# Mixture-of-experts attention block: another order of work in the attention stage, and fewer register instructions in the expert stage

## The reference, cut to what matters

```
x = x + conv(groupnorm(x))                      # untouched by the change
t = x as (8, 256, 64)
n = layernorm(t)
t = t + softmax((n Wq' + bq)(n Wk' + bk)' / 8) (n Wv' + bv)
n = layernorm(t)
p = softmax(n gate_w + gate_b); the two largest, divided by their sum, are the shares
t = t + sum over the two experts e of share_e * (silu(n w1[e]) * (n w2[e])) w3[e]
```

## Time and profile before

| what | before |
|---|---|
| median of 3 runs | 532.63 us (531.43 to 534.22) |
| profiled execution | 531.87 us |
| its span, first to last instruction | 530.1 us |
| mean granted clock of TensorE | 0.761 of full speed |
| busy: TensorE, VectorE, ScalarE, GpSimd | 373.8, 272.1, 181.0, 165.5 us |

### The profile page before, as it was taken

How to read it: one execution, slowest core, us unless ns; L and a number is a source line. 1 busy time by engine, 2 the same in 40 slices (tenths; PEclk the granted TensorE clock), 3 DMA queues, 4 the chain that set the end, 5 groups by cost and what they waited for, 6 DMA issues and landing times.

```text
span 530.1 us, 8806 instructions
## 1 busy us (share of the span) xinstructions
PE 373.8 (71%) x2739; PEld 201.0 (38%) x2739; DVE 272.1 (51%) x559; ACT 181.0 (34%) x401; POOL 165.5 (31%) x179
## 2 busy tenths in 40 slices
PE   0799999999999999998476261705046666666670
PEld 0533534344443434332355150604024444444440
DVE  3569877997789787789325433223112222122222
ACT  3746557464656565630133120101012222222220
POOL 2443232324233242300102435151503333333331
PEclk9969999999999999999786767555555555555555
DMA  9599999896949577670000000000022322232224
GB/s 290 203 215 287 220 279 264 219 222 158 214 126 211 139 172 184 154 206 1 0 0 2 13 8 16 6 16 5 21 65 70 74 72 69 66 71 68 71 48 119
DMA packets 55093, 61.52 MB, mean 116 GB/s; under 512 B 22900, under 2 KB 35244, under 8 KB 54928
## 3 DMA queue, kind: packets, MB, share of 16 engines
q1 hardware_dynamic: 52528, 58.93, 43.4%
q0 software_dynamic: 2528, 2.14, 1.3%
HBM read 11.95 MB, written 11.83 MB: 45 GB/s over the span
## 4 chain that ended last, share of the span: by engine, by line
SPq 13%; PE 12%; issue 9%; DMA 5%; DVE 5%; POOL 5%; ACT 1%; POOLq 0%; ACTq 0%
POOL rows L1226 4%; DMA x_in<-rows 4%; SPq L989 3%; SPq L988 3%; SPq L992 3%; SPq L985 2%; SPq L993 2%; PE ps_go L1388 2%; PE ps_s L1434 2%; PE ps_xv L1350 1%; PE ps_go L1443 1%; DVE ln_out L1030 1%; PE ps_xv L1426 1%; POOL ln_rstd L1211 1%; DMA both<-parts 1%
## 5 line engine op out<-in xcount | busy, mean ns | idle before, releaser
L684 DVE TENSOR_TENSOR prod<-ps_t,a_rep 128x1024 f32<-128x1024 f32 x128 | 152.0, 1218 | 35.8 <-PE ps_t L384 34.9
L384 PE MATMUL ps_t<-b,vt 32*128 32x512 f32 x512 | 75.4, 659 | 1.9 <-DVE prod L684 1.9
L1235 POOL DMA_INDIRECT parts<-y_sb,x_in x47 | 45.7, 972 | 92.6 <-ACT y_sb L1308 92.2
L791 POOL TENSOR_TENSOR a<-a,mask 128x512 f32<-128x512 f32 (+1 forms) x40 | 47.0, 1177 | 83.9 <-ACT a L544 81.9
L404 PE MATMUL ps_d<-prod,keep 128*32 128x512 f32 x512 | 69.1, 612 | 0.3 <-DVE prod L684 0.2
L1426 PE MATMUL ps_xv<-attention_pack,x_in 128*128 128x128 f32 x47 | 22.3, 475 | 57.9 <-DMA x_in<-rows 57.9
L325 PEld LDWEIGHTS ps_m<-om_r,sel 128*128 128x128 f32 x193 | 29.0, 188 | 75.5 <-ACT mask L522 28.2
L1140 DVE COPY xs<-ps_xv 128x128 f32<-128x128 f32 x47 | 13.7, 292 | 79.3 <-PE ps_xv L1426 79.3
L1300 ACT ACTIVATE gated<-ps_s 128x128 f32<-128x128 f32 x47 | 13.0, 278 | 108.3 <-PE ps_p L1435 108.3
L1226 POOL DMA_INDIRECT rows<-stage,slot_at x32 | 31.6, 988 | 57.6 <-DVE stage L1106 35.7
L325 PE MATMUL ps_m<-om_r,sel 128*128 128x256 f32 x193 | 49.3, 334 | 0.0
(11 more groups left out here) (151 smaller groups left out, 530.3 us busy)
## 6 DMA issues: line engine op xcount, KB each, us to landing
a_rep<-a SPq DMA_DIRECT2D x128, 256.0 KB, 4.8
rows<-blank SPq DMA_DIRECT2D x8, 1056.0 KB, 7.8
w_in<-in_experts SPq DMA_DIRECT2D x47, 96.0 KB, 1.9
a_rep<-a SPq DMA_DIRECT2D x32, 128.0 KB, 3.4
x_in<-rows SPq DMA_DIRECT2D x47, 33.0 KB, 1.8
x_in<-rows SPq DMA_DIRECT2D x47, 32.0 KB, 1.7
start<-in_start SPq DMA_DIRECT2D x1, 1344.0 KB, 7.3
both<-parts SPq DMA_DIRECT2D x4, 256.0 KB, 3.6
```

The source lines that it names most:

```text
L384: mm = pe.matmul(out, vt[par][r, v % 2, :, :, :].rearrange("p j y c -> p (j y c)"), b[par][r, pair_taps(v // 2), :].rearrange("p t x -> p ...
L684: dve.tensor_tensor(p[:, :, :], t[:, :, :], a_rep[par][:, ms, pair_taps(v // 2), :].rearrange("p m t x -> p m (t x)"), ALU.mult).then_inc( ...
L791: pool.tensor_tensor(v, v, mask[(PAIRS * par + k) % 2][:, 0:wide, :], ALU.mult).then_inc(a_done, 1)
L1235: pool.indirect_dma_start(out=parts[:, :], out_offset=bass.IndirectOffsetOnAxis(ap=x_in[b][:, C + ROW - 1:C + ROW].bitcast(I32), axis=0), ...
```

## The change

The rounds are gone. Each engine has a list written by hand, in which a couple's phases are interleaved more finely. GpSimd computes the four roots of s = 0 first, and the root of s = 1 for couple q + 1 ahead of the scatters of couple q. Moments, variances and roots have a place for each couple, so `power` waits no longer for `ln_apply`. The two copies into `stage` are ScalarE's (`keep`). `qkv` and `project_qkv` are split in two, `copy_qk` and `copy_v`, `project_qk` and `project_v`, so that each half has its own place in a list. The scatters of the rows have no bounds check; those of the results take theirs from a register that is set once. SyncE reads four steps' values with one load for each row of the table (`table_values`, `LOADS` = 4), and without the check of their range. The order of SyncE's three loads within a step is the same, and they were all SyncE's before.

```diff
-    ROUNDS = COUPLES + 2
+    LOADS = 4
...
-        moments = [sb(f"ln_moments{s}", [P, K, 2]) for s in two]
+        moments = [sb(f"ln_moments{s}", [P, COUPLES, K, 2]) for s in two]
...
+        def table_values(eng, line, s, most):
+            ahead = min(LOADS, STEPS - s)
+            return nc.values_load_multi_w_load_instructions(
+                table[line:line + 1, s:s + ahead], engines=(eng.engine,), min_val=0, max_val=most,
+                skip_runtime_bounds_check_because="the table's entries are clamped where they are made")[1]
...
         @block.sync
         def _(sp):
+            sp.wait_ge(tab_done, 1)
+            sp.wait_ge(placed, 16 * 2 * TT)
             for s in range(STEPS):
                 b = s % RING
-                if s == 0:
-                    sp.wait_ge(tab_done, 1)
-                    sp.wait_ge(placed, 16 * 2 * TT)
-                expert_row = sp.value_load(table[1:2, s:s + 1], min_val=0, max_val=(EXPERTS - 1) * P)
+                if s % LOADS == 0:
+                    at_rows, at_expert = table_values(sp, 0, s, DEAD), table_values(sp, 1, s, (EXPERTS - 1) * P)
+                row = at_rows[s % LOADS]
                 if positive(s - RING + 1):
                     sp.wait_ge(y_ps, s - RING + 1)
-                sp.dma_start(w_in[b][:, :], w_rows[bass.ds(expert_row, P), :]).then_inc(w_here[b], 16)
-                row = sp.value_load(table[0:1, s:s + 1], min_val=0, max_val=DEAD)
+                sp.dma_start(w_in[b][:, :], w_rows[bass.ds(at_expert[s % LOADS], P), :]).then_inc(w_here[b], 16)
                 if positive(s - RING + 1):
                     sp.wait_ge(sent[b], 16 * (uses(s) - 1))
...
```

VectorE's list (`ln` is stats, moments and variance; `largest` score_max and score_negate; `residual` invert_sums and add_values; `choose` gate_logits to top_hot; `place` top_slot and top_share):

```diff
+            ln(0, 0)
+            ln(0, 1)
+            ln_apply(0, 0)
+            ln(0, 2)
+            ln_apply(0, 1)
+            ln(0, 3)
+            largest(0)
+            ln_apply(0, 2)
+            residual(0)
+            ln(1, 0)
+            largest(1)
+            ln_apply(1, 0)
+            ln_apply(0, 3)
+            choose(0)
+            residual(1)
+            ln(1, 1)
+            largest(2)
+            ln_apply(1, 1)
+            place(0)
+            choose(1)
+            residual(2)
+            ln(1, 2)
+            largest(3)
+            ln_apply(1, 2)
+            place(1)
+            choose(2)
+            residual(3)
+            ln(1, 3)
+            place(2)
+            ln_apply(1, 3)
+            choose(3)
+            place(3)
             step_table()
```

GpSimd:

```diff
             def power(s, q):
                 pool.wait_ge(ln_stat[s], LN_STEPS * (q + 1))
-                if positive(q):
-                    pool.wait_ge(ln_done[s], q)
...
             def place(q):
-                pool.wait_ge(ln_done[1], q + 1)
-                for i in two:
-                    k = K * q + TPI * i
-                    pool.tensor_copy(stage[:, k:k + TPI, :, 0:C], spread(normed[1][:, :, i, :], 2, 2)).then_inc(staged, 1)
                 pool.wait_ge(staged, 2 * (q + 1))
...
-                            in_=stage[:, k, w, :], in_offset=None, bounds_check=DEAD - 1, oob_is_err=False)\
+                            in_=stage[:, k, w, :], in_offset=None)\
                             .then_inc(placed, 16)
...
-                    in_=y_sb[b][:, :], in_offset=None, bounds_check=2 * TT * P - 1, oob_is_err=False)\
+                    in_=y_sb[b][:, :], in_offset=None, bounds_check=last_part, oob_is_err=False)\
...
+            for q in range(COUPLES):
+                power(0, q)
+            power(1, 0)
+            power(1, 1)
+            place(0)
+            power(1, 2)
+            place(1)
+            power(1, 3)
+            place(2)
+            place(3)
+            last_part = pool.snap(2 * TT * P - 1)
             for s in range(STEPS):
                 send(s)
```

ScalarE's new `keep`, and its list from couple 0's attention on (`weights` is exps, `turned_weights` copy_p):

```diff
+            def keep(q):
+                act.wait_ge(ln_done[1], q + 1)
+                for i in two:
+                    k = K * q + TPI * i
+                    act.activation(stage[:, k:k + TPI, :, 0:C], spread(normed[1][:, :, i, :], 2, 2), ACT.Copy)\
+                       .then_inc(staged, 1)
...
+            weights(1)
+            turned(1, 0)
+            turned_weights(1)
+            copy_qk(2)
+            copy_v(2)
+            keep(0)
+            gap_exps(0)
+            turned(0, 3)
+            copy_qk(3)
+            weights(2)
+            turned(1, 1)
+            turned_weights(2)
+            copy_v(3)
+            keep(1)
+            gap_exps(1)
...
```

TensorE's list (after it, as before, `counts()` and the steps):

```diff
+            turn(0, 0)
+            project_qk(0)
+            project_v(0)
+            scores(0)
+            turn(0, 1)
+            project_qk(1)
+            turn_p(0)
+            values(0)
+            scores(1)
+            project_v(1)
+            turn(0, 2)
+            project_qk(2)
+            turn(1, 0)
+            project_v(2)
+            turn_p(1)
+            gate_product(0)
+            values(1)
+            scores(2)
+            rank(0)
...
+            scores(3)
+            rank(1)
+            turn(1, 2)
+            turn_p(3)
+            gate_product(2)
+            values(3)
+            rank(2)
+            turn(1, 3)
+            gate_product(3)
+            rank(3)
             counts()
```

More of the change, by code:

```diff
@@ L844, in token_stage @@
         stats = [sb(f"ln_stats{s}", [P, K, 6]) for s in two]
-        moments = [sb(f"ln_moments{s}", [P, K, 2]) for s in two]
-        var_eps = [sb(f"ln_var{s}", [P, K]) for s in two]
-        rstd = [sb(f"ln_rstd{s}", [P, K]) for s in two]
+        moments = [sb(f"ln_moments{s}", [P, COUPLES, K, 2]) for s in two]
+        var_eps = [sb(f"ln_var{s}", [P, COUPLES, K]) for s in two]
+        rstd = [sb(f"ln_rstd{s}", [P, COUPLES, K]) for s in two]
         normed = [sb(f"ln_out{s}", [P, TPI, 2, C]) for s in two]
@@ L966, in token_stage @@
         w_rows = d["experts"]
-        def stages(r):
-            return [q if 0 <= q < COUPLES else None for q in (r, r - 1, r - 2)]
+        def table_values(eng, line, s, most):
[3 more added lines that the diff above has]
+                skip_runtime_bounds_check_because="the table's entries are clamped where they are made")[1]
         def uses(s):
@@ L1014, in ln_moments @@
                 for k in range(K):
-                    dve.bn_aggr(moments[s][:, k, :], stats[s][:, k, :]).then_inc(ln_stat[s], 1)
+                    dve.bn_aggr(moments[s][:, q, k, :], stats[s][:, k, :]).then_inc(ln_stat[s], 1)
             def ln_variance(s, q):
                 dve.wait_ge(ln_stat[s], LN_STEPS * q + 2 * K)
-                dve.tensor_scalar(var_eps[s][:, :], moments[s][:, :, 1], LN_EPS, None, ALU.add)\
+                dve.tensor_scalar(var_eps[s][:, q, :], moments[s][:, q, :, 1], LN_EPS, None, ALU.add)\
                    .then_inc(ln_stat[s], 1)
@@ L1029, in ln_apply @@
                     i, t = divmod(k, TPI)
-                    op = dve.tensor_scalar(normed[s][:, t, i, :], t_tok[:, K * q + k, :], moments[s][:, k, 0:1],
-                                           rstd[s][:, k:k + 1], ALU.subtract, ALU.mult)
+                    op = dve.tensor_scalar(normed[s][:, t, i, :], t_tok[:, K * q + k, :], moments[s][:, q, k, 0:1],
+                                           rstd[s][:, q, k:k + 1], ALU.subtract, ALU.mult)
                 op.then_inc(ln_done[s], 1)
@@ L1153, in finish @@
                 dve.tensor_tensor(tokens, added[q][:, :, :], tokens, ALU.add).then_inc(finished, 1)
-            dve.wait_ge(pack_in, 16)
[L1156 to L1185, removed]
@@ new lines, in ln, with largest, residual, choose @@
+            def ln(s, q):
+                ln_stats(s, q)
+                ln_moments(s, q)
+                ln_variance(s, q)
+            def largest(q):
+                score_max(q)
+                score_negate(q)
+            def residual(q):
+                invert_sums(q)
+                add_values(q)
+            def choose(q):
+                gate_logits(q)
+                top_largest(q)
+                top_index(q)
+                top_hot(q)
+            def place(q):
+                top_slot(q)
+                top_share(q)
@@ L1208, in power @@
                 pool.wait_ge(ln_stat[s], LN_STEPS * (q + 1))
-                if positive(q):
-                    pool.wait_ge(ln_done[s], q)
-                pool.tensor_tensor(rstd[s][:, :], var_eps[s][:, :], minus_half[:, :], ALU.pow)\
+                pool.tensor_tensor(rstd[s][:, q, :], var_eps[s][:, q, :], minus_half[:, :], ALU.pow)\
                     .then_inc(ln_pow[s], 1)
             def place(q):
-                pool.wait_ge(ln_done[1], q + 1)
-                for i in two:
-                    k = K * q + TPI * i
-                    pool.tensor_copy(stage[:, k:k + TPI, :, 0:C], spread(normed[1][:, :, i, :], 2, 2)).then_inc(staged, 1)
                 pool.wait_ge(staged, 2 * (q + 1))
@@ L1260, in turned, with copy_qk @@
                 act.activation(xt[s][:, :], ps_x[s], ACT.Copy).then_inc(x_done[s], 1)
-            def qkv(q):
+            def copy_qk(q):
```

(40 more changed lines are left out.)

## The result

The change brought 532.05 us (four runs of the kernel before beside it) to 453.14 us (452.07 to 454.22, four runs): ratio 0.8511, 95% interval 0.8476 to 0.8546. The profiled execution took 453.77 us.

A forecast was written before the change was run, and what follows sets the result against it. The prediction saw two stages behind the convolution, each held by one queue: GpSimd's (attention) and SyncE's (expert). 531.9 - 41.6 (attention) - 34.3 (expert steps) - 0.5 (last scatter to first x) = 455.5 us, range 448 to 461.

The forecast's parts named there:

- First scatter: Attention stage: the first row scatter on GpSimd would start at 292.4 us, with bounds of 288.5 and 298.
- Rival 1: Expert stage: TensorE's clock returns to 2.4 GHz, 1.74 us a step, 446 us in all; chance 0.20.
- The three steps between places: Attention stage, GpSimd: times between the starts of the four couples' groups of eight row scatters, first 14.5 us.
- The table: End of the attention stage: the step table's writing stays hidden under the last eight scatters; otherwise SyncE would wait for it.
- The scatters' check: Attention stage: dropping the row scatters' bounds check counts 0, bounded by 0.2 us each way for 24 scatters, 5 us.
- the near end of the attention stage: Attention stage: largest gain, -46 us, with the first scatter at 288.5 and the last chain within 10.14 us.
- rival 3: Expert stage: SyncE's loads aren't merged, only the checks go; 2.13 us a step, 466 us in all; chance 0.07.
- The step: Expert stage: 1.95 us a step, four steps holding one 7.8 us round of the six-buffer ring; 46 steps 91.4 us, -34.3.
- The send's register move: Expert stage, GpSimd: 0.03 us saved per send, lying before its launch, so worth 0.
- 2: Expert stage: with 40% more traffic per us landings take 1 us more; 2.2 us a step, 467 us; chance 0.14.
- 4: Attention stage: row scatters slow down beside VectorE's work, 7.4 us more, 463 us in all; chance 0.06.
- 5: Expert stage: slower than before, as the ring's round grows; at a round of 16 us, 548 us; chance 0.03.

The follow-up runs named there:

- e5: The changed kernel with each of the last two roots behind the fifth of the eight scatters before it, not behind all; 448.93 us.
- e4: The changed kernel with eight buffers for x, weights and results instead of six; 441.96 us.
- e3: The changed kernel with one value a register load instead of four, still without the check; 462.66 us.

## Why the prediction was right

The forecast was 455.5 us, the median 453.1. The mechanism of both stages is the one forecast. That the total is off by 2.4 us only is partly luck: the attention stage gave 3.2 us more than forecast and the steps 1.4 us less, and inside the first scatter's term larger errors cancelled in part. Point by point:

*First scatter: the term that was furthest off.* "So rank(0) ends at 291.3 + 3.1 - 4.4 = 290.0. VectorE then does pick to share without a wait". The timeline of the changed kernel, PE's end of rank(0) and VectorE after it:

```profile
284.47 0.41 PE L1470 MATMUL ps_go<-attention_pack 128*128 128x64 f32 x2
...
285.34 1.22 DVE L1039 TENSOR_REDUCE score_max<-ps_s 128x4 f32<-128x1024 f32 x1
...
286.70 0.98 DVE L1033 TENSOR_SCALAR ln_out<-t_tok,ln_moments,ln_rstd 128x64 f32<-128x64 f32 x4
...
287.60 0.28 DVE L1095 TENSOR_TENSOR pick<-hot,ps_go 128x128 f32<-128x128 f32 x1
...
288.72 0.17 DVE L1109 TENSOR_TENSOR stage<-gap_exp,stage 128x4 f32<-128x4 f32 x1
```

Rank(0) was over at 284.9, 5.1 us earlier, and 6.0 if one takes off that the stage was entered 0.9 later. Most of that goes with the clock. From its first product of the stage to the end of rank(0) TensorE was busy 20.75 us and idle 2.70 (261.43 to 284.88), at a granted clock of 0.89; before it was busy 22.22 and idle 8.70 (260.54 to 291.46), at 0.68. The new list adds 3.1 us of products ahead of rank(0), so at the old clock it would have been busy 25.3: the clock gave back some 4.6 us, an estimate from these figures. The filled waits are 6.0 us, where I had counted 4.4. Four products of one kind show what the clock is worth, before at 0.50 and now at 1.00:

```profile
284.84 2.05 PE L1350 MATMUL ps_xv<-xt,attention_pack 128*128 128x256 f32 x4
```

```profile
285.58 1.13 PE L1408 MATMUL ps_xv<-xt,attention_pack 128*128 128x256 f32 x4 [0.47 <-ACT xt L1285]
```

The prediction took the old clock for its sum, and the faster one only for its lower bound. Rival 1, a higher clock, was looked for in the expert stage alone; it came in this stretch, where TensorE was idle less. On the other side, pick starts at 287.60 and not behind rank(0) at once: the score maximum of couple 2 and an apply stand ahead of it in VectorE's own list, 2.7 us that the prediction didn't have. The two errors have opposite signs, 6.0 us too late and 2.7 too early, and that they cancel in part is luck. The term was 292.4 against 289.86, and against 289.0 with the later entry taken off.

*The three steps between places* were 14.5, 11.2 and 11.5 against 14.13, 11.14 and 11.48. e5 shows their reason: with the root among the scatters, the first and the last are 11.4 and 10.2. *The table* stayed hidden, as SyncE waited for the last scatter's landing. *The copies* on ScalarE leave no mark in these steps. *The scatters' check* was taken as 0 and is 0.5 us. Two side sums of the prediction are slightly off and nothing rests on them: by its terms the near end of the attention stage is -46.9, not -46, and rival 3 gives 465.4, not 466.

*The step.* 1.95 and half of the extras, 91.4 us, against 92.8. The round itself is right to 0.04 us (7.8 and 7.84); the extras above 46 x 1.96 are 2.6 us, not 1.7, and some sends do land late (one of 3.34 us at 357.47). SyncE's own step, 1.68 in the forecast, is 1.51 + 2 x 0.33 / 4 = 1.67. TensorE needs 1.74 us a step (54.12 us for 31.2 steps), not 1.85. *The send's register move* is still there, 47 times at 29 ns, although its value is set once, so the 0.03 us a send that the prediction calls saved are not; it had put their worth at 0.

*Rivals.* 1: the clock stayed at 0.50 throughout the stage, even at 92% busy in e4. 2: the mean round is 4 x 2.02 = 8.07 us, 0.2 above the one of the chain shown; single sends landed in up to 3.3 us, but no microsecond was added. 3: the loads were merged (24 of them), and unmerged ones would have cost 9.5 us (e3, 8.1 of them in the steps), near the 10 forecast. 4: the scatters took 0.96 in the median with VectorE at work beside them, and four of the 32 took 1.03 to 1.18. The Trainium skill, "GPSIMD Engine Reference", section "Key points", has GpSimd contend for its SBUF interfaces with VectorE instructions that run in a 2-port perf mode or have two SBUF inputs. Beside `hot` in `top_hot`, which has two, one scatter took 0.96 (at 291.35) and one 1.03 (at 320.29), so the trace doesn't settle it. 5: the round binds, but at 7.84 us, not 14.6.

The 200 ns a register of the Trainium skill ("Runtime: NRT & Kernel Launch", section "Instruction fetch mechanics") don't hold for these loads from SBUF: one value takes 0.27 us, four 0.30, eight 0.53. An estimate by that page would be 0.8 us for four.

## What to carry to other kernels

On an engine with its own list, a short instruction that others wait for goes ahead of long ones that nobody waits for yet; here that alone gave 28 us, and it can go in between them too. When a queue that issues loads gets faster, work out the round of its ring (issue, landing, use, send, landing) over the steps it may run ahead: it gave the new step within 4% here, and says what one buffer less costs and how many more still help. Where the queue itself stays the bound, add the extras of the old trace in full: e3 suggests it, with 0.10 us a step that its forecast left out.

## What the runs showed that I had not expected

- Register loads from SBUF on SyncE: 0.27 us for one value, 0.30 for four, 0.527 for eight. From one value to four costs next to nothing, from four to eight 0.23, so eight save little more than four.
- The range check behind a register load cost three times what merging the loads saved with six buffers: 24.4 us against 8.1 over 46 steps.
- With TensorE 92% busy in the expert stage of e4 the granted clock stayed 0.50. In the convolution of the changed kernel, 60 to 250 us, it was 1.00 with TensorE busy 99%.
- The untouched convolution stage ended 4.2 us apart between executions (256.9 to 261.1). None of the runs tells why.
- With the new order TensorE's granted clock was higher in the attention stage. In every profile of it the clock from 275 to 285 us was 1.00, where the old order had 0.76 to 0.83.
